# Where the q and k parts lie in memory, who loads the first stack, and when batch 1 is projected

## The reference

```python
qkv = x @ W_qkv_v.T @ W_qkv_u.T              # rank 32, 128 -> 3 * 128
q, k, v = jnp.split(qkv, 3, axis=-1)         # 16 heads of 8
scores = jnp.einsum('bhtd,bhsd->bhts', q, k) * (1 / sqrt(8))
attn = jax.nn.softmax(scores, axis=-1)
y = jnp.einsum('bhts,bhsd->bhtd', attn, v)
y = y.reshape(B, T, 128) @ W_o_v.T @ W_o_u.T
```

## Time and profile before

| what | value |
|---|---|
| median of 3 runs | 702.95 us (701.66 to 705.38) |
| the profiled execution, its own time | 705.56 us |
| its span on the core | 703.8 us |
| PE busy | 572.7 us (81%) |
| DVE busy | 453.7 us (64%) |
| ACT busy | 373.3 us (53%) |
| POOL busy | 144.4 us (21%) |

### The profile page before, as it was taken

How to read it: one execution, slowest core, us unless ns; L and a number is a source line. 1 busy time by engine, 2 the same in 40 slices (tenths; PEclk the granted TensorE clock), 3 DMA queues, 4 the chain that set the end, 5 groups by cost and what they waited for, 6 DMA issues and landing times.

```text
span 703.8 us, 11663 instructions
## 1 busy us (share of the span) xinstructions
PE 572.7 (81%) x3560; PEld 205.5 (29%) x3560; DVE 453.7 (64%) x815; ACT 373.3 (53%) x816; POOL 144.4 (21%) x228
## 2 busy tenths in 40 slices
PE   2976999644689898888988889888898868679992
PEld 2543444332211221222212222122222244344441
DVE  5631344265689889888898888988882638233442
ACT  2211344233217788777887778877787732124330
POOL 2470355433300000000000000000000002604452
PEclk9995999866658999999999999999999988979996
DMA  9994233113410000001000010000000000111114
GB/s 231 325 349 125 79 87 85 45 49 118 146 50 35 1 2 27 22 1 47 1 26 22 1 47 2 1 2 1 3 2 2 0 1 16 47 30 55 50 43 130
DMA packets 52295, 40.56 MB, mean 58 GB/s; under 512 B 4905, under 2 KB 49598, under 8 KB 52240
## 3 DMA queue, kind: packets, MB, share of 16 engines
q1 hardware_dynamic: 49168, 35.58, 17.0%
q0 software_dynamic: 3072, 4.28, 1.9%
HBM read 26.85 MB, written 14.88 MB: 59 GB/s over the span
## 4 chain that ended last, share of the span: by engine, by line
PE 55%; DVE 17%; issue 11%; DMA 6%; ACT 4%; POOL 2%; SPq 2%; another core or an unknown queue 2%; ACTq 0%; POOLq 0%; DVEq 0%
PE bank L1190 15%; DVE rowmax L913 10%; PE pair L1169 10%; PE pair L1060 7%; PE bank L1181 7%; PE bank L1077 4%; PE pair L1069 3%; ACT arena L673 2%; DMA xe<-rows 2%; PE pair L984 1%; PE bank L1048 1%; POOL rows L466 1%; PE bank L1198 1%; PE pair L976 1%
## 5 line engine op out<-in xcount | busy, mean ns | idle before, releaser
L913 DVE TENSOR_REDUCE rowmax<-pair 128x1 f32<-128x1024 f32 x256 | 301.0, 1219 | 37.9 <-PE pair L1169 35.9
L673 ACT ACTIVATE arena<-bank 128x512 f32<-128x512 f32 x512 | 269.6, 602 | 72.8 <-PE bank L1181 72.6
L1169 PE MATMUL pair<-k_stack,q_stack 48*128 48x512 bf16 x512 | 162.3, 406 | 31.6 <-DVE rowmax L913 22.4
L1181 PE MATMUL bank<-q_stack,k_stack 51*128 51x512 bf16 x512 | 163.3, 387 | 16.6 <-ACT arena L673 8.0
L1190 PE MATMUL bank<-arena 128*32 128x512 f32 x1024 | 137.2, 608 | 0.0
L1169 PEld LDWEIGHTS pair<-k_stack,q_stack 48*128 48x128 bf16 x512 | 33.0, 95 | 173.7 <-DVE rowmax L913 141.8
L473 POOL DMA_INDIRECT y<-yb,slot_token x64 | 63.0, 984 | 99.7 <-ACT yb L586 81.2
L863 DVE TENSOR_TENSOR arena<-pair,arena 128x256 f32<-128x256 f32 x64 | 27.2, 425 | 82.5 <-ACT arena L581 59.9
L1060 PE MATMUL pair<-w_exp,xeT 128*64 x128 | 69.3, 624 | 0.5 <-ACT xeT L576 0.5
L1062 PE MATMUL pair<-w_exp,xeT 128*64 128x512 f32 x128 | 69.3, 624 | 0.0
L500 POOL TENSOR_TENSOR mpart<-zeros,rowmax 128x16 bf16<-128x16 f32 x16 | 3.6, 223 | 261.9 <-DVE rowmax L913 261.9
(11 more groups left out here) (135 smaller groups left out, 535.6 us busy)
## 6 DMA issues: line engine op xcount, KB each, us to landing
xe<-rows SPq DMA_DIRECT2D x64, 66.0 KB
w_exp<-in_r_gate SPq DMA_DIRECT2D x4, 1024.0 KB
w_exp<-in_r_up SPq DMA_DIRECT2D x4, 1024.0 KB
w_exp<-in_r_down SPq DMA_DIRECT2D x8, 512.0 KB
rows<-empty_row SPq DMA_DIRECT2D x1, 2112.0 KB, 11.7
rows<-empty_row SPq DMA_DIRECT2D x32, 66.0 KB
xnT<-y SPq DMA_DIRECT2D x8, 256.0 KB, 3.6
q_parts<-arena SPq DMA_DIRECT2D x12, 128.0 KB, 2.7
```

The source lines that it names most:

```text
L673: nc.scalar.activation(prob[c % 2 * GH + HEAD_OF_STEP[k]], ring_bank("score", STEPS * u + i), ACT.Exp, scale=SCALE).then_inc(prob_ready, 1)
L913: nc.vector.tensor_reduce(rowmax[u % 2][:, m:m + 1], pair[j % 2][:, :], AX_X, ALU.max).then_inc(smax_read, 1)
L1169: ins = nc.tensor.matmul(pair[j % 2][:, part * BANK:(part + 1) * BANK], q_stack[r][rows, half, l, t * P:(t + 1) * P], k_stack[r][rows, l, ...
L1181: nc.tensor.matmul(ring_bank("score", i), k_stack[r][rows, l, c * P:(c + 1) * P], q_stack[r][rows, half, l, :], start=True, stop=True).the ...
```

## The change

There are four edits.

1. In memory, each row of 512 tokens of a q or k part is a piece of 1 KB by itself, with a gap of 64 bytes (`DRAM_GAP`) behind it. Before, four such pieces of q and two of k stood end to end, so that a partition of a stack was loaded in one run of 4 KB. Now it is four runs of 1 KB.
2. k is projected, split and stored before q (`qk` is inverted in `project_qk`, `store_parts` and `part_stores`).
3. `stack_loads(queue, g, a)` replaces the body of `load_stacks`. The half a = 0 of stack 0 is issued by SP, the half a = 1 by ACT, after `part1(3)` and ahead of batch 1's rows; for this ACT waits for `stacks_cleared` and the four `parts_stored`.
4. `project_qk(4..7)` move from ahead of the first maxima to behind blocks 2 to 5; `project_v(2)` and `(3)` move from behind blocks 8 and 9 to behind 11 and 12. Ahead of block 0 PE waits for all of `xnT` instead.

```diff
+DRAM_GAP = 32
-        q_dram = nc.dram_tensor("q_parts", (3, P, 2 * SEQ), BF16, kind="Internal").ap()
-        k_dram = nc.dram_tensor("k_parts", (3, 2 * P, SEQ), BF16, kind="Internal").ap()
+        q_dram = nc.dram_tensor("q_parts", (3, P, 4, QW + DRAM_GAP), BF16, kind="Internal").ap()
+        k_dram = nc.dram_tensor("k_parts", (3, 2 * P, 2, QW + DRAM_GAP), BF16, kind="Internal").ap()
-        part_stores = lambda i: 1 if i // 2 % 2 else 3
+        part_stores = lambda i: 3 if i // 2 % 2 else 1
+        def stack_loads(queue, g, a):
+
+            r, row = g % STACKS, HALF * a
+            for part, n in enumerate(Q_OF_K):
+                rows = slice(row, row + n * HD)
+                row += n * HD
+                q = q_dram[0:n, (2 * g + a) * HD:(2 * g + a + 1) * HD, :, 0:QW].rearrange("n d x t -> (n d) x t") if n == 1 else \
+                    q_dram[0:n, (2 * g + a) * HD:(2 * g + a + 1) * HD, :, 0:QW]
+                queue.dma_start(q_stack[r][rows, :, :, :].rearrange("p a l t -> p (a l) t"), q).then_inc(stack_loaded[r], 16)
+                k = k_dram[part, (2 * g + a) * 2 * HD:(2 * g + a + 1) * 2 * HD, :, 0:QW].rearrange("(d l) x t -> d (l x) t", l=2)
+                queue.dma_start(k_stack[r][rows, :, :].rearrange("p l (x t) -> p (l x) t", t=QW),
+                                k.unsqueeze(0).broadcast_to([n, HD, 4, QW])).then_inc(stack_loaded[r], 16)
...
-                    if i // 2 % 2:
-                        sp.dma_start(k_dram[:, b * P:(b + 1) * P, half * QW:(half + 1) * QW].rearrange("c p t -> p c t"),
+                    if i // 2 % 2 == 0:
+                        sp.dma_start(k_dram[:, b * P:(b + 1) * P, half, 0:QW].rearrange("c p t -> p c t"),
...
-                            dst = q_dram[c, b * HALF:(b + 1) * HALF, half * 2 * QW:(half + 1) * 2 * QW]
-                            sp.dma_start(dst.rearrange("r (h t) -> r h t", t=QW), part_sb[i % 4][:, c, :])\
+                            dst = q_dram[c, b * HALF:(b + 1) * HALF, 2 * half:2 * half + 2, 0:QW]
+                            sp.dma_start(dst, part_sb[i % 4][:, c, :])\
...
-                load_stacks(0)
+                load_stacks(0, halves=(0,))
                 load_stacks(1)
...
                 part1(3)
+                act.wait_ge(stacks_cleared, 1)
+                for i in range(4):
+                    act.wait_ge(parts_stored[i], 16 * part_stores(i))
+                stack_loads(nc.scalar, 0, 1)
                 transposed(1, 2, 4)
...
-                    b, qk, half = i // 4, i // 2 % 2, i % 2
+                    b, qk, half = i // 4, 1 - i // 2 % 2, i % 2
...
                 sequence_rows(1)
-                for i in range(4, 8):
-                    project_qk(i)
+                pe.wait_ge(xnT_ready, 2 * QUADS)
                 pe.wait_ge(v_sb, 2)
...
-                    if j in (8, 9):
-                        pe.wait_ge(part0_sb, j - 1)
-                        project_v(j - 6)
+                    if 2 <= j < 6:
+                        project_qk(j + 2)
+                    if j in (11, 12):
+                        pe.wait_ge(part0_sb, j - 4)
+                        project_v(j - 9)
```

More of the change, by code:

```diff
@@ L367, in store_parts, with load_stacks @@
                         for c in range(3):
-                            dst = q_dram[c, b * HALF:(b + 1) * HALF, half * 2 * QW:(half + 1) * 2 * QW]
-                            sp.dma_start(dst.rearrange("r (h t) -> r h t", t=QW), part_sb[i % 4][:, c, :])\
+                            dst = q_dram[c, b * HALF:(b + 1) * HALF, 2 * half:2 * half + 2, 0:QW]
+                            sp.dma_start(dst, part_sb[i % 4][:, c, :])\
                                 .then_inc(parts_stored[i % 4], 16)
-                def load_stacks(g):
-                    r = g % STACKS
-                    for a in range(2):
-                        row = HALF * a
-                        for part, n in enumerate(Q_OF_K):
-                            rows = slice(row, row + n * HD)
-                            row += n * HD
-                            q = q_dram[0:n, (2 * g + a) * HD:(2 * g + a + 1) * HD, :]
-                            k = k_dram[part, (2 * g + a) * 2 * HD:(2 * g + a + 1) * 2 * HD, :].rearrange("(d l) t -> d (l t)", l=2)
-                            sp.dma_start(q_stack[r][rows, :, :, :].rearrange("p a l t -> p (a l t)"), q).then_inc(stack_loaded[r], 16)
-                            sp.dma_start(k_stack[r][rows, :, :].rearrange("p l t -> p (l t)"),
-                                         k.unsqueeze(0).broadcast_to([n, HD, 2 * SEQ])).then_inc(stack_loaded[r], 16)
+                def load_stacks(g, halves=(0, 1)):
+                    for a in halves:
+                        stack_loads(nc.sync, g, a)
                 def load_m(u):
```

## The result

The changed kernel takes 714.41 us (median of 4 runs, 713.30 to 715.56), the kernel before 703.55 us (median of 4, 701.66 to 705.38). The ratio is 1.0152, with a 95% interval of 1.0135 to 1.0170: 10.9 us slower. The forecast was 707.5 us, 4.5 us slower, with a range from 699 to 710, so the direction was right, and the loss is more than twice the one forecast. The profiled execution took 713.3 us, its span is 711.5 us, 7.7 us more than the traced execution of the kernel before; where the rest of the 10.9 lies is said at the end.

The account below looks back on a forecast made before the run. The prediction took stack 0's landing, set by the first engine's backlog, to bound the start of the maxima. Its terms, 0 + 0 + 1.2 + 2.9 + 0.4 = +4.5 us on a median of 702.95, gave 707.5 us, range 699 to 710.

Parts of the forecast that it names:

- What bounds the start: Attention's start: only stack 0's landing starts the maxima; a load runs on n engines, always the same first ones.
- k before q: Stores of batch 0's parts: the last store lands at 164.2 to 165.3 against 164.56; 0, bounds -0.4 and +0.7.
- ACT's half: Loading of stack 0: same first engines, so their backlog, not the issue, sets the landing; worth 0.
- Pieces of 1 KB: Stack loads: four times as many packets on the same engines; +1.2 us, the middle of 0 and 2.5.
- The clock at the landing: First block of maxima: landing slips behind the clock's fall at 180.23, so the block takes 1.03 us; +0.4.
- The projections among the maxima: Behind blocks 2 to 5: four projections of 0.95 us lose their cover and delay DVE; +2.9 us, bounds 0 and 3.8.
- signs of being wrong: Landing before 176, share well above 0.3 from 167 to 172, PEclk 1.00 from 190 to 210, or scores awaiting `mT`'s load.
- Later stacks and `mT`: After stack 0: stack 2's loads and `load_m(0)` come later but stay hidden, the latter by 2 us; 0.
- The clock did not rise: Rival, projections between maxima: clock rises to 1.00 from about 190 and stays; 702.6 us, no change; chance 0.18.
- Other engines: Rival, stack 0's load: ACT's half runs on other engines, landing at 173.6; -2.4, 700.5 us; chance 0.13.
- spread: Rival, stack loads: smaller pieces spread a load over all engines, landing at 171.1; -4.2, 698.8 us; chance 0.07.
- Queues fill: Rival, load issue: full queues hold ACT beyond 177 or delay `load_m(0)`; adds about 3, 710.5 us; chance 0.08.

Follow-up runs that it names:

- a1: Changed kernel with batch 1's q and k projected ahead of the first maxima again, its values behind blocks 8 and 9: 708.45 us, 1.0018 of the kernel before.
- b1: Kernel before with only the 1 KB pieces and gap, all of stack 0 on SP, q first, projections ahead of the maxima: 707.21 us, 1.0030 of the kernel before.

## Why the prediction was wrong

**What bounds the start: right.** Stack 0's landing starts the maxima, and when the loads are spread over more engines the maxima start 4.7 us earlier. That loads ran on the same few engines was inferred from shares of 0.19 and 0.13 and is now shown: the same bytes in the same runs, only with 8 instead of n outermost, gave 0.40. The loads that have 8 outermost in the kernel before show it too: SP issues them at 167.65, 171.28 and 174.88, and the share is 0.42 from 168.75 to 169.25, 0.39 from 172.25 to 173.00 and 0.39 from 175.75 to 176.50, under the 0.50 of eight engines and far under the 0.69 of eight beside the three, so the three are among the eight. Between and behind these stretches it is back at 0.20 (174.80 to 175.70) and 0.19 (176.50 to 179.20), with loads of two stacks in the queue. So the shares fit the outermost dimension in all three sizes of this case (0.19 for three, 0.13 for two, 0.39 to 0.42 for eight), and loads queued together had the same few engines. Which of the 16 they were no trace here shows; "the first ones" was the author's name for them. The 1.7 us between issue and first packet is shown: with the issue at 164.64 the DMA share is 0.00 up to 166.20 and 0.21 from there to 166.50.

**k before q, 0: right.** The last store of a part lands at 164.16 (162.01 + 2.15) against 164.56, a difference within the spread of 13.1 to 14.3 us behind the first projection that both orders have, and behind it the landing takes as long with either order.

**ACT's half, 0: a little too low.** Moving the issues did not make the landing earlier, as forecast, but the prediction had no term by which it could make it later. It cost 0.7 us alone and 0.6 on top of the pieces. That the same engines were now also given stack 1 sooner is a likely reason and not tested. The rest of the +1.9 us of its ratio stays open.

**Pieces of 1 KB, +1.2 (0 to 2.5): in the range, 1.7 and 1.6 us measured.** The prediction's sum from the stores' rate, 22.8 GB/s for an engine, gave +1.7, and the two engines of the tail moved 22.5 each. The halving to 1.2, for fear that the stores had been held down by memory, was not needed. In the stack loads' own windows the traces have 26.5 GB/s for an engine with runs of 4 KB against 22.5 with pieces, 18% more.

**The clock at the landing, +0.4: the size right, the reason wrong for this kernel.** The first block takes 1.04 us instead of 0.61 where the granted clock is 0.50. (The traces give the clock as a share, not in GHz. In the kernel before bf16 matmuls of 512 columns start 0.22 us apart at 1.00, at 378.66 and 378.88, so 2.3 columns a ns; at 0.50 two take 1.03 us of which the second has 0.63, so they start 0.40 apart, 1.3 columns a ns. The 2.4 and 1.2 GHz named ahead of the result can be checked no further than against this estimate.) With the pieces alone a later landing slips behind the fall, as predicted. In the changed kernel, and with edit 4 alone, there was no fall: batch 1's projections, during which the clock had risen before, no longer stand ahead of the landing, and it was 0.50 all along. Put those back (a1), and the first block takes 0.61 us at 181.73.

**The projections among the maxima, +2.9: the step that failed.** It measured 7.0. The mechanism was right, four gaps behind blocks 2 to 5 at the low clock, but "a projection of 0.95 us" was not. It was worked out as 3.78 us for four from the earlier trace rows. That row comes from a view whose stretch ended at 172.0 us, though its heading in this document says otherwise, and counts only what had started by then. The timeline of the kernel before over a stretch that holds them all:

```profile
150.60 4.74 PE L1126 MATMUL bank<-xnT,w_qkv 128*128 128x512 f32 x8
...
168.92 5.90 PE L1126 MATMUL bank<-xnT,w_qkv 128*128 128x512 f32 x8
```

and the group of this line over the whole span (line, operation, count | busy us, mean ns | idle):

```profile
L1126 PE MATMUL bank<-xnT,w_qkv 128*128 128x512 f32 x16 | 10.6, 826 | 0.0
```

Eight projections are written as eight matmuls and leave sixteen records: two for each. "x4" was two projections, in 3.78 us, 1.9 each at 0.50. The 5.90 us are all four of batch 1, part of it at 1.00. With 2.00 us for a projection behind 0.96 for a block, the gap is 2.97 - 1.23 = 1.74, what the trace shows.

The check that the prediction made on itself should have caught it. It reckoned a value projection at 2.07 us and found its gap of 1.74 right; but `project_v` multiplies four times 128 columns in float32, as many columns as a projection of q or k has. That two jobs of 512 float32 columns take 2.07 and 0.95 us at the same clock should have raised a doubt. So should the bf16 matmuls beside them: a block's two of 512 columns take 0.96 us in the changed kernel's chain, 0.48 each, and a float32 projection of 512 columns takes 2.00 there, 4.2 times that, where 0.95 would have been twice. None of the prediction's signs of being wrong appeared; of its signs of being right two did not come as written, the gap of 0.7 and the idle time of over 8 us ahead of block 0 (7.38).

With the measured sizes the sum is 0 + 0.6 + 1.7 + 7.0 + 0.4 = 9.7, and from the last store the first scores were 9.9 us later (56.22 against 46.34). Of the 5.2 us that the prediction's sum lacks, 4.1 are the projections.

**Later stacks and `mT`, 0: right.** Behind the first scores nothing moved: 371.57 us before, 371.51 in the changed kernel, to the second FFN's gate.

**The rivals.** The clock did not rise among the projections. Windows of the changed kernel, columns as in the earlier trace rows:

```profile
183.00:200.00 17.00, 14.89 (x24) 2.90 (x24) 10.03 (x9) 6.64 (x12) 8.85 (x8) 0.50 0.23 75
200.00:227.00 27.00, 23.77 (x72) 6.46 (x73) 22.63 (x20) 7.61 (x19) 1.32 (x6) 0.50 0.25 80
228.00:245.00 17.00, 16.22 (x112) 3.44 (x111) 16.21 (x15) 14.20 (x29) 1.10 (x5) 1.00 0.03 10
```

PE was busy 14.89 of 17 us there and was granted 0.50, and so on to 226, when unit 0 had been running for over 5 us. "Other engines" and "spread" are out by the share of 0.19. "Queues fill" happened (4.67 us for one issue, ACT held to 171.4), and held up nothing that the maxima waited for, since the landing came later still; whether it has a part in the 0.6 us of ACT's half is not known. That a queue takes only so many packets is best seen where SP issues all pieces of 1 KB (b1): six issues, half a stack, took 4.49 us from 164.56 and then, with loads queued up, 6.30, 6.56 and 6.28 us (169.05 to 188.19), against 3.83 and 3.61 in the kernel before. The fullest engine's 136 pieces at 22.5 GB/s take 6.2, an estimate, so SP issued no faster than they left.

**What stays open.** By the ratio the changed kernel is 9.5 to 12.0 us slower, and the 9.9 us up to the first scores lie within that. The two traced executions differ by 7.7 us only: in the changed kernel's, 0.4 us less passed before the last store, and the second FFN, in which no edit lies, took 119.61 us from its gate to the end of the span against 121.33. I have no cause for that difference, nor for the 1.3 us by which ACT's half alone is slower than its trace shows.

## What to carry to other kernels

Before dividing a row's time by its count, ask what one count is and whether the view's stretch holds all of the group; then compare the result with another row of the same work, here float32 columns against float32 columns. Work that stands under a wait is free only there: once moved between steps that an engine at its limit waits for, it costs its full length less the slack, each time. And when a load takes long and the DMA share is a few sixteenths, look at its outermost dimension before changing pieces or queues: two words of layout gained 5 us here, where of the three edits to the loads one gained nothing and two cost 0.6 and 1.7.

## What the runs showed of the hardware that was not expected

Two queues that issued the same kind of load shared the same three engines (12.6% of the 16 engines' time for SP's queue and 7.6% for ACT's from 173 to 176 us, 0.20 together): ACT's six issues, done 2.6 us sooner behind the last store, made the landing 0.6 us later. An engine moved pieces of 1 KB at 22.5 GB/s and runs of 4 KB at 26.5, where two were busy; at shares of 0.19 and 0.20 most windows have 64 to 72 GB/s with pieces and 66 to 82 with long runs. Issuing can stall: with pieces of 1 KB and few engines single issues took 4.67, 2.29 and 1.93 us, against 0.28 to 0.83 for most before, where one took 3.15. And late in the attention the granted clock fell to 0.50 for 10.2 us in one execution of a kernel and not in the next, with PE busy 7.44 of 10 us ahead of it in the first and 7.61 in the second; a single profiled execution can be 4 us off for that alone.
